# Two output products of a cross attention computed before the block change instead of after it

## The reference

```python
x = x + cross_attention(layernorm(x), context)     # 8 heads of 64; out @ Wo + bo
x = x + self_attention(layernorm(x))               # causal, 8 heads, 2 latent key/value heads
x = x + experts(layernorm(x))                      # shared FFN + top 2 of 8 experts, hidden 1024
```

## Time and profile before

| | us |
|---|---|
| median of 3 runs | 1599.76 (1598.81 to 1599.98) |
| profiled execution, whole | 1589.36 |
| its span, first to last instruction | 1587.5 |
| TensorE busy | 1516.4 (96%) |
| mean granted TensorE clock | 0.985 |

### The profile page before, as it was taken

The page is one execution under the profiler, slowest core; times in us unless marked ns, Lnnn a source line. Parts: engine busy times, 40 slices in busy tenths (PEclk is TensorE's granted clock), DMA queues, the critical chain, the costliest instruction groups (busy, mean ns, idle before and its releaser), DMA issues. The chain is left out here.

```text
span 1587.5 us, 25168 instructions
## 1 busy us (share of the span) xinstructions
PE 1516.4 (96%) x10038; PEld 1221.4 (77%) x10039; DVE 625.6 (39%) x953; ACT 686.3 (43%) x1121; POOL 720.5 (45%) x563
## 2 busy tenths in 40 slices
PE   7999999999999999999999999888699979999997
PEld 5678888888888888888888888745367768877876
DVE  4134434533534533632732731732654522222222
ACT  3244544544543544544543643504254424444621
POOL 3113822931941841851751651537200175688651
PEclk9999999999999999999999999999899989999999
DMA  6111021021021021021111111052000475467511
GB/s 212 60 54 59 2 87 44 18 87 34 28 87 34 28 87 34 28 75 39 35 60 54 34 41 54 1 194 92 15 1 1 153 226 146 140 190 195 146 35 35
DMA packets 56164, 116.90 MB, mean 74 GB/s; under 512 B 11072, under 2 KB 15232, under 8 KB 56064
## 3 DMA queue, kind: packets, MB, share of 16 engines
q1 hardware_dynamic: 46480, 98.17, 18.6%
q0 software_dynamic: 4816, 8.41, 2.8%
q10 hardware_dynamic: 4768, 8.91, 2.0%
HBM read 94.19 MB, written 22.33 MB: 73 GB/s over the span
## 5 line engine op out<-in xcount | busy, mean ns | idle before, releaser
L282 POOL TENSOR_TENSOR ctx_l<-stage,ctx_h 128x1024 fp32r<-128x1024 f32 x62 | 147.0, 2393 | 482.3 <-ACT ctx_h L630 482.3
L344 PE MATMUL ps_p<-wv,ctx_h 128*128 128x512 f32 x1024 | 323.7, 397 | 10.4 <-DVE ctx_l L700 9.4
L344 PE MATMUL ps_p<-ctx_h,wk 128*128 128x512 f32 x1024 | 331.0, 394 | 0.0
L738 DVE TENSOR_TENSOR s_top<-ps_s,s_top 128x512 f32<-128x512 f32 x192 | 121.2, 684 | 338.8 <-ACT s L599 338.8
L344 PEld LDWEIGHTS ps_p<-wv,ctx_h 128*128 128x128 f32 x1024 | 188.0, 189 | 53.7 <-issue 10.0
L344 PEld LDWEIGHTS ps_p<-ctx_h,wk 128*128 128x128 f32 x1024 | 192.2, 188 | 42.6 <-issue 1.2
L344 PE MATMUL ps_p<-wv,ctx_l 128*128 128x512 f32 x512 | 200.4, 391 | 0.0
L344 PE MATMUL ps_p<-ctx_l,wk 128*128 128x512 f32 x512 | 199.5, 390 | 0.0
L581 ACT ACTIVATE vt<-ps_p 128x512 f32<-128x512 f32 x128 | 76.4, 598 | 274.9 <-PE ps_p L344 213.7
L599 ACT ACTIVATE s<-ps_s 128x512 f32<-128x512 f32 x256 | 133.0, 602 | 61.1 <-PE ps_s L397 36.7
L575 ACT ACTIVATE kT<-ps_p 128x512 f32<-128x512 f32 x128 | 76.5, 598 | 176.7 <-PE ps_p L344 176.6
(11 more groups left out here) (255 smaller groups left out, 2253.9 us busy)
## 6 DMA issues: line engine op xcount, KB each, us to landing
stage<-in_ctx_dram SPq DMA_DIRECT2D x64, 512.0 KB, 4.0
raw_u<-in_up_dram SPq DMA_DIRECT2D x32, 512.0 KB, 4.2
stage<-in_down_dram SPq DMA_DIRECT2D x16, 512.0 KB, 4.1
raw_e<-in_down_dram SPq DMA_DIRECT2D x16, 512.0 KB, 4.1
rows_scratch<-wxo SPq DMA_DIRECT2D x25, 256.0 KB, 2.6
wxo<-rows_scratch ACTq DMA_DIRECT2D x23, 256.0 KB, 3.3
s<-in_x_dram SPq DMA_DIRECT2D x2, 1024.0 KB, 11.5
q_scratch<-s SPq DMA_DIRECT2D x2, 1024.0 KB, 4.6
```

What stands on the lines that cost most here:

```text
L282: nc.gpsimd.tensor_tensor(lo, raw, hi, ALU.subtract).then_inc(done, 1)
L344: mm = nc.tensor.matmul(out, w(c), m(c), start=(c + k == 0), stop=(c == DC - 1 and k == 2))
L738: ins = nc.vector.tensor_tensor(top[:, p, e], bank, top[:, p, e], ALU.max)
```

## The change

`ps_p` becomes a pair of banks, `pair_ps`, allocated outside of both blocks. In the last sequence's softmax, TensorE makes the output product of sequence 0 after the spread of pair 2 (before that of pair 3), into the first bank, and that of sequence 1 after the values of pair 1, into the second. In the self attention the two banks stand in the place of banks 6 and 7; TensorE marks both as filled at once and begins with the product of sequence 2. x of sequences 0 and 1 goes to a tile of its own, `x_soon`, loaded by SyncE at the end of the cross attention, with a wait for it before the output weights are loaded; the first load of x in the self attention is of sequences 2 and 3 only. `x2` is now a list of views on the two tiles.

```diff
+XE = 2
-        ps_p = ctx.enter_context(nc.psum_tensor("ps_p", [P, 2, 512], F32))
+        ps_p = pair_ps
...
+            sp.dma_start(x_soon[:, :, :], x_ap[0:XE].rearrange("s t d -> t s d")).then_inc(x_early, 16)
             sp.wait_ge(zeroed, 16 * (ROWS - B * T // P))
+            sp.wait_ge(x_early, 16)
             sp.wait_ge(l_done, LASTB)
             sp.dma_start(wxo[:, :, :], wxo_ap.rearrange("(c p) n -> p c n", p=P)).then_inc(wxo_in, 16)
...
+            def output_early(s):
+
+                pe.wait_ge(wxo_in, 16)
+                pe.wait_ge(o_early, 16)
+                pe.wait_ge(v_copied, B * MT)
+                rows = stage[:, :, :, :].rearrange("p a c (h t) -> p (a c) h t", t=T)
+                for p in range(PAIRS):
+                    mm = nc.tensor.matmul(ps_p[:, s, :], rows[:, s, p, :], wxo[:, p, :], start=(p == 0), stop=(p == PAIRS - 1))
+                return mm
+
             for p in range(1, PAIRS):
                 spread_max(LASTB, p)
+                if p == 2:
+                    output_early(0)
             for p in range(PAIRS):
                 values(LASTB, p)
+                if p == 1:
+                    output_early(1)
...
-        banks = [ctx.enter_context(nc.psum_tensor(f"bank{i}", [P, 512], F32)) for i in range(8)]
+        banks = [ctx.enter_context(nc.psum_tensor(f"bank{i}", [P, 512], F32)) for i in range(6)] \
+            + [pair_ps[:, i, :] for i in range(2)]
...
             for s in range(B):
-                pool.wait_ge(x_got[s // HB], 16)
-                nc.gpsimd.tensor_tensor(x2[:, s, :], x2[:, s, :], bo[:, :], ALU.add).then_inc(xb_done, 1)
+                pool.wait_ge(x_early if s < XE else x_got[s // HB], 16)
+                nc.gpsimd.tensor_tensor(x2[s], x2[s], bo[:, :], ALU.add).then_inc(xb_done, 1)
...
             pe.wait_ge(wxo_in, 16)
-            for s in range(HB):
+            for s in range(2):
+                seen[6 + s].append(f"out{s}")
+                pe.sem_inc(filled[6 + s], 1)
+            for s in range(2, HB):
                 cross_out(s)
...
             for n in range(2):
-                seqs = slice(n * HB, (n + 1) * HB)
-                act.dma_start(x2[:, seqs, :], x_ap[seqs].rearrange("s t d -> t s d")).then_inc(x_got[n], 16)
+                seqs = slice(n * HB or XE, (n + 1) * HB)
+                act.dma_start(x_late[:, seqs.start - XE:seqs.stop - XE, :], x_ap[seqs].rearrange("s t d -> t s d")).then_inc(x_got[n], 16)
...
+        pair_ps = ctx.enter_context(nc.psum_tensor("pair_ps", [P, 2, 512], F32))
+        x_soon = ctx.enter_context(nc.sbuf_tensor("x_soon", [P, XE, D], F32))
+        x_early = ctx.enter_context(nc.semaphore("x_early"))
...
-        x2 = ctx.enter_context(nc.sbuf_tensor("x2", [P, B, D], F32))
+        x_late = ctx.enter_context(nc.sbuf_tensor("x_late", [P, B - XE, D], F32))
+        x2 = [x_soon[:, s, :] if s < XE else x_late[:, s - XE, :] for s in range(B)]
```

More of the change, by code:

```diff
@@ L60, in cross_attention @@
 def cross_attention(nc, x_ap, ctx_ap, wq_ap, wk_ap, wv_ap, wxo_ap, q_dram, o_dram, rows_dram, wxo, wxo_in, stage, on,
-                    o_early):
+                    o_early,
+                    x_soon, x_early, pair_ps):
     with ExitStack() as ctx:
@@ L840, in self_attention @@
 def self_attention(nc, x_ap, bo_ap, wxo, wxo_in, wq_ap, wkd_ap, wvd_ap, wku_ap, wvu_ap, wo_ap, wg_ap, up_ap, down_ap,
-                   o_dram, o_early, stage, on, x2, xn3, logits, hu, hd, lu, ld, rowT_h, rowT_l, gT_h, gT_l, raw_in, hi_done, lo_done, one):
+                   o_dram, o_early, stage, on, x2, xn3, logits, hu, hd, lu, ld, rowT_h, rowT_l, gT_h, gT_l, raw_in, hi_done, lo_done, one,
+                   x_late, x_early, pair_ps):
     with ExitStack() as ctx:
@@ L970, in bank @@
         def bank(name):
-            return banks[PLACE[name][0]][:, :]
+            i = PLACE[name][0]
+            return banks[i][:, :] if i < 6 else banks[i]
         def await_filled(eng, name):
@@ L1455, in add @@
                 await_filled(dve, name)
-                copy(nc.vector.tensor_tensor(x2[:, s, :], bank(name), x2[:, s, :], ALU.add), name)
+                copy(nc.vector.tensor_tensor(x2[s], bank(name), x2[s], ALU.add), name)
                 await_copied(dve, name)
                 nc.vector.memset(hold[:, :], 0.0)
-                link(nc.vector.bn_stats(stats[:, par, :], x2[:, s, :]))
+                link(nc.vector.bn_stats(stats[:, par, :], x2[s]))
                 nc.vector.memset(hold[:, :], 0.0)
@@ L1467, in norm @@
                 dve.wait_ge(rstd_done, n + 1)
-                nc.vector.tensor_scalar(xn3[:, s, :], x2[:, s, :], mv[:, par, 0:1], rstd[:, par, :], ALU.subtract,
+                nc.vector.tensor_scalar(xn3[:, s, :], x2[s], mv[:, par, 0:1], rstd[:, par, :], ALU.subtract,
                                         ALU.mult).then_inc(xn_done, 1)
@@ L1518, in _ @@
                     await_filled(dve, f"dn{late}")
-                    copy(nc.vector.tensor_tensor(x2[:, late, :], bank(f"dn{late}"), x2[:, late, :], ALU.add), f"dn{late}")
+                    copy(nc.vector.tensor_tensor(x2[late], bank(f"dn{late}"), x2[late], ALU.add), f"dn{late}")
                 await_filled(dve, f"lg{s}")
@@ L1524, in experts @@
 def experts(nc, room, stage, on, up_ap, down_ap, out_ap, rows_dram, meta_dram, x2, xn3, logits, hu0, hd0, lu0, ld0,
-            rowT_h, rowT_l, gT_h, gT_l, raw_in, hi_done, lo_done):
+            rowT_h, rowT_l, gT_h, gT_l, raw_in, hi_done, lo_done, pair_ps):
     with ExitStack() as ctx:
@@ L1575, in experts @@
         slot_i = sb("slot_i", [P, 2, NT], U32)
-        up_ps = ctx.enter_context(nc.psum_tensor("up_ps", [P, NH, 512], F32))
+        up_ps = pair_ps
         gT_ps = ctx.enter_context(nc.psum_tensor("gT_ps", [P, NH, 4, P], F32))
@@ L1634, in store_out @@
                 sp.wait_ge(y_copied, t + (AHEAD + 1))
-                sp.dma_start(out_ap[t], x2[:, t, :]).then_inc(out_stored, 16)
+                sp.dma_start(out_ap[t], x2[t]).then_inc(out_stored, 16)
             load_raw(1)
@@ L1888, in add_shared @@
                 dve.wait_ge(down_done, t + 1)
-                x2t = x2[:, bass.ds(t, 1), :].rearrange("p o d -> p (o d)")
-                nc.vector.tensor_tensor(x2t, down_ps[:, :], x2t, ALU.add).then_inc(y_copied, 1)
+                nc.vector.tensor_tensor(x2[t], down_ps[:, :], x2[t], ALU.add).then_inc(y_copied, 1)
             def spread(ap):
@@ L1989, in perceiver_block @@
         o_early = ctx.enter_context(nc.semaphore("o_early"))
-        cross_attention(nc, x, ctx_t, xq, xk, xv, xo, q_dram, o_dram, rows_dram, wxo, wxo_in, stage, on, o_early)
-        x2 = ctx.enter_context(nc.sbuf_tensor("x2", [P, B, D], F32))
+        pair_ps = ctx.enter_context(nc.psum_tensor("pair_ps", [P, 2, 512], F32))
+        x_soon = ctx.enter_context(nc.sbuf_tensor("x_soon", [P, XE, D], F32))
+        x_early = ctx.enter_context(nc.semaphore("x_early"))
+        cross_attention(nc, x, ctx_t, xq, xk, xv, xo, q_dram, o_dram, rows_dram, wxo, wxo_in, stage, on, o_early,
+                        x_soon, x_early, pair_ps)
+        x_late = ctx.enter_context(nc.sbuf_tensor("x_late", [P, B - XE, D], F32))
+        x2 = [x_soon[:, s, :] if s < XE else x_late[:, s - XE, :] for s in range(B)]
         xn3 = ctx.enter_context(nc.sbuf_tensor("xn3", [P, B, D], F32))
@@ L2007, in perceiver_block @@
         self_attention(nc, x, xbo, wxo, wxo_in, sq, skd, svd, sku, svu, so, gate, up, down, o_dram,
-                       o_early, stage, on, x2, xn3, logits, hu, hd, lu, ld, rowT_h, rowT_l, gT_h, gT_l, raw_in, hi_done, lo_done, one)
+                       o_early, stage, on, x2, xn3, logits, hu, hd, lu, ld, rowT_h, rowT_l, gT_h, gT_l, raw_in, hi_done, lo_done, one,
+                       x_late, x_early, pair_ps)
         experts(nc, wxo, stage, on, up, down, out, rows_dram, meta_dram, x2, xn3, logits, hu, hd, lu, ld,
-                rowT_h, rowT_l, gT_h, gT_l, raw_in, hi_done, lo_done)
+                rowT_h, rowT_l, gT_h, gT_l, raw_in, hi_done, lo_done, pair_ps)
 def kernel(**inputs):
```

## The result

| kernel | median us | runs | lowest to highest |
|---|---|---|---|
| before | 1599.54 | 20 | 1598.81 to 1600.04 |
| changed | 1596.56 | 20 | 1594.84 to 1598.81 |

The ratio is 0.9981, with a 95% interval of 0.9974 to 0.9988: 3.0 us less, between 1.9 and 4.2. The forecast was 1598.3, 1.5 us less than the median then known (1599.76), with a range of 1595.0 to 1600.8: the direction and the range held, the gain was twice the forecast one.

The account below looks back on a forecast made before the run. TensorE was taken to bound the cross attention's end, and the chain from x's landing through bias and sum the self attention's start. +1.8 for moved products and -3.3 for the earlier chain made -1.5: 1598.3 us, range 1595.0 to 1600.8.

Parts of the forecast that it names:

- The bound: Self attention's start: the chain of x landing, bias, sum, statistics, power sets its end; the products' 13.97 us lie beside it.
- Part 1, the first product: Cross attention, TensorE's gap after the second spread: made at half clock from 1006.85, it costs only 0.7 to 1.3 us.
- rival (e): First product's gap: the clock holds or returns early, 0 - 3.3 = -3.3 us, 1596.5; chance 0.08.
- Part 1, the second product: Cross attention, before pair 2's values: takes 3.49 us, makes them 3.6 to 4.2 late, swallows the 1.83 wait for GpSimd.
- the net of part 1: Cross attention's end: both moved products together cost 1.8 us, range 0 to +2.4.
- Part 2: End of the cross attention: loading x of two sequences early costs nothing, with over 30 us of cover.
- Part 3: Self attention's start: the first bias waits for bo alone, so the chain starts at 5.5 us, not 8.8: minus 3.3.
- The sum: At 1076.66, after the last sequence's sum: +1.8 - 3.3 = -1.5 us, giving 1598.3.
- rival (a): Self attention's start: TensorE's gap drops the clock, which may then hold for later transposes: another -1.7, 1596.6; chance 0.22.
- (b): Self attention's start: after the same gap the clock stays down for all four steps, +9.0 us, 1608.8; chance 0.05.
- (c): Self attention's start: bo lands like x, so the chain starts as before, +1.8 us, 1601.6; chance 0.08.
- (d): Self attention's start: bo lands in 2.1 us, as alone, -3.3 more, -4.8 in all, 1595.0; chance 0.10.

Follow-up runs that it names:

- x early alone: Against the kernel before: x of two sequences loaded early, all four output products left at the start of the self attention; 1594.83 us, ratio 0.9970; again 1594.91.
- the products alone: Against the kernel before: two output products made in the cross attention, x loaded as before; 1599.37 us, ratio 1.0003.
- x and bo: Against the kernel before: x of two sequences and the bias row bo loaded in the cross attention, no product moved; 1591.71 us, ratio 0.9951.
- the filled gap: Changed kernel plus five unread products in TensorE's gap before the self attention's first transposes; 1596.18 us, ratio 0.9982 to the kernel before.

## Why the prediction was right, and by how much it was off

**The bound.** Right: the start of the chain, not the products. x early alone has all the gain, the products alone have none.

**Part 1, the first product.** This is the step that was mis-sized most. The place was right (1006.72), its price wrong: forecast 0.7 to 1.3 us, measured 0. Two things failed. The clock was taken to be at half there, as in the earlier trace rows. That was special to the one trace: the clock fell there before 1007, but in the kernel before's second profile the mean clock of 1004 to 1010 is 0.95, so it fell only after 1009. In the profiles without a product in that place (before twice, x early alone twice, x and bo) the mean clock of 1000 to 1040 is 0.91; with one it is 0.99 or 1.00 in six of eight, and 0.96 in two (the products alone and the changed kernel's second profile, 5.29 us for the product in each). So with work moved into the gap the clock mostly stayed up, which the prediction had as rival (e) with a chance of 0.08. And the values of pairs 0 and 1 were taken to follow each other in 7.0 us. With the clock up they don't, as ScalarE's exponentials set when those of pair 1 start: not before 1015.2, and TensorE waits 1.22 us for them. The wait's row could not stand in the trace of before, where the half clock hid it, but the exponentials' own line (1014.10) could have been used. The two errors pull against each other. For a clock that holds, the prediction has a net near 0 for both products, and the exponentials make 0.8 of it. In the two executions where the clock fell during the first product, the case nearest to the assumed one, the values of both pairs took 7.21 us without a wait and the net was 1.1 us, still under 1.8.

**Part 1, the second product.** The mechanism was right, to the wait of 1.83 us that it swallows, and so was the size. Of the 3.6 to 4.2 us by which the values of pair 2 were to be late, 0.7 to 1.3 came from the first product and 2.9 from this one; measured were 3.0, all from this one. So the net of part 1, 0.9 where +1.8 was taken, is off by the first product's price. It is the larger part of the error of the sum.

**Part 2.** Right: the output weights are issued 2.0 us later, the outputs at 957.41 as before, both long ahead of 1006.72.

```profile
951.23 0.45 SPq L264 DMA_DIRECT2D x_soon<-in_x_dram  x1
955.03 0.38 SPq L268 DMA_DIRECT2D wxo<-in_xo_dram  x1
957.41 0.37 SPq L271 DMA_DIRECT2D stage<-o_scratch  x1
```

**Part 3.** Right in kind and nearly in size: bo lands after 4.9 us instead of 5.4, the bias starts 5.0 us into the block (up to 5.3 in other kernels), -3.8 instead of -3.3. The load of x stayed off the path. The first small load behind bo, 6.0 to 6.2 us with it, took 2.2 to 2.9 where bo was gone. That agrees with the turn-taking between queues that the Trainium skill states in "DMA: Bandwidth & Descriptors", section "Queues, rings and completion order": what delayed it stood in its own queue, and the loads of x, in the other, were there both times.

**The sum.** +0.9 - 3.8 = -2.9 at the transposes behind the last sum, measured 1073.78 against 1076.66, where -1.5 was forecast; the medians differ by 3.0. Both terms were off to the same side. That the measured 1596.56 is nearly the 1596.6 of rival (a) and the 1596.5 of rival (e) is chance: the 1.7 us that (a) adds came as 0.7 and (e) has neither the 0.9 of the second product nor the 3.8 of bo. The range held because it took in (e), and not because the clock of the forecast was the one that ran.

**The rivals.** (a) The gap brought the clock down, TensorE fell behind by some 2 us, and no one waited: shown by the rows and by the filled gap. Whether the clock then holds at 1070 to 1077 was left open; it fell but came back 5 us earlier in the trace, 0.7 us of further gain there. Such gains don't last: at the first up products (1165.36, before 1165.99) only 0.6 us of the 3.6 was left, as the clock stood at half at 1155 to 1160 in this execution, and in the second profile of the changed kernel, where it didn't, the same product came at 1163.78. The second profile of the kernel before has it at 1167.86. They move from one execution to the next and lie in the spread of the runs. The premise beside it, that the gap of 2.2 us before the block's first product leaves the clock up, holds only for the one trace: in seven of the thirteen profiled executions, the second of the kernel before among them, the clock fell between 1039 and 1042, behind this gap of 2.2 to 2.4 us, and was back by 1046. It costs nothing as long as no sum waits for these products. (b) The clock didn't stay down: it was back 4.5 us after work resumed. (c) and (d) are out by the landing of bo. The Trainium skill's "TensorE: Matmul & The Clock Gate", section "HAM oscillation — how this bites in real kernels", warns of repeated falls between bursts; here one fall followed the gap and none came within the steps, from 1057 to 1069 at 1.00.

## What to carry to other kernels

Before work is moved out of a stage, ask what its first consumer waits for: here the sum waited for a load, and moving the load alone was worth more than moving the load and the work. Work fits a gap for free only up to the next wait behind it: the first product found a gap and a wait to end in, the second pushed the path. When a load is taken off the path, the next operand beside it becomes the bound, and the same treatment of a 2 KB row gave another 3 to 5 us. And a clock that one trace shows up or down at a place may stand otherwise in the next execution: take a second profile before a term is built on it.

## What the runs showed of the hardware

The load of one row to all 128 partitions, 256 KB in SBUF, took 4.9 to 5.4 us at the start of the block, beside the loads of x. A store of 256 KB from SBUF to DRAM, issued at 950.31, took 2.1 us; how much of the difference is the spreading and how much the other loads isn't separated. Taken out of there, it let x's 512 KB land in 4.1 to 4.3 us instead of 6.2 to 6.5.

With work of 3.6 us put into TensorE's gap at 1006 the granted clock stayed up in six of eight profiled executions, and it fell in all five without. Where it stayed up, the first product cost nothing: the values behind it ran at full clock, 3.71 us for a pair, where those of pairs 0 and 1 in the kernel before took 8.75 together. At the block's start, after a gap of 2.2 to 2.4 us without matmuls, the clock fell in seven of thirteen executions and stayed up in six, of the same kernel too (the kernel before: once up, once down).
